# Causal attention: values 256 columns wide, in pieces behind the four long steps, and one turned buffer per query tile

## The reference, cut to what matters

```python
qkv = einsum('bnd,ed->bne', xn, w_qkv)          # xn: layernorm of x; 16 heads of 64
q, k, v = split(qkv, 3)                          # q is scaled by 64 ** -0.5
sim = einsum('bhid,bhjd->bhij', q, k)            # 1024 queries by 1024 keys
sim = where(j > i, -big, sim)                    # causal
attn = softmax(sim)
out = einsum('bhij,bhjd->bhid', attn, v)
x = x + einsum('bne,de->bnd', out, w_out) + b_out
```

## Time and profile before

| | |
|---|---|
| median of 3 executions | 3728.84 us (3725.52 to 3732.86) |
| profiled execution, its own time | 3723.46 us |
| span of the profile, first to last instruction | 3721.7 us |
| mean granted TensorE clock | 0.966 of full speed |
| busy over the span: PE, PEld, DVE, ACT, POOL | 3207.6, 2018.8, 2102.9, 2087.8, 1727.1 us |
| line 1528 (values), PE MATMUL | 4608 instructions, 307.8 us busy, 278 ns each |
| the stretch of `causal_attention`'s units | about 1608 to 2875 us of the span |

### The profile page before, as it was taken

How to read it: one execution, slowest core, us unless ns; L and a number is a source line. 1 busy time by engine, 2 the same in 40 slices (tenths; PEclk the granted TensorE clock), 3 DMA queues, 4 the chain that set the end, 5 groups by cost and what they waited for, 6 DMA issues and landing times. The chain is left out here.

```text
span 3721.7 us, 77077 instructions
## 1 busy us (share of the span) xinstructions
PE 3207.6 (86%) x28486; PEld 2018.8 (54%) x28612; DVE 2102.9 (57%) x4204; ACT 2087.8 (56%) x3388; POOL 1727.1 (46%) x1348
## 2 busy tenths in 40 slices
PE   6599999858889888579999999999998588899885
PEld 4222222635566666346666666666665355666663
DVE  4200000468887777455555555555556688777773
ACT  2499999335555555345555555555554355555552
POOL 1100000168888888223333333333332688888882
PEclk9799999979999999889999999999999799999998
DMA  1122221021111111000000000000000211111111
GB/s 34 22 37 39 36 38 25 7 83 38 34 35 35 35 34 30 14 9 10 6 6 8 6 6 8 6 8 6 6 8 2 85 35 34 35 35 35 34 31 32
DMA packets 124408, 95.75 MB, mean 26 GB/s; under 512 B 80448, under 2 KB 100544, under 8 KB 123968
## 3 DMA queue, kind: packets, MB, share of 16 engines
q1 hardware_dynamic: 122784, 89.41, 11.0%
q10 hardware_dynamic: 1440, 3.80, 0.3%
HBM read 22.90 MB, written 2.10 MB: 7 GB/s over the span
## 5 line engine op out<-in xcount | busy, mean ns | idle before, releaser
L1703 POOL TENSOR_SCALAR e<-e,inv 128x768 f32<-128x768 f32 (+7 forms) x512 | 375.0, 745 | 845.2 <-DVE inv L1599 845.2
L1668 ACT ACTIVATE e<-e,nmax 128x768 f32<-128x768 f32 (+7 forms) x512 | 396.0, 774 | 434.4 <-DVE e L1594 431.2
L530 ACT ACTIVATE e<-slot 128x1024 f32<-128x1024 f32 x512 | 472.6, 1091 | 38.5 <-PE slot L466 38.5
L1594 DVE TENSOR_SCALAR_CACHE_REDUCE e<-slot 128x768 f32<-128x768 f32 (+7 forms) x512 | 375.7, 753 | 161.4 <-PE slot L1504 161.4
L1515 PE MATMUL slot<-ident,e 128*128 128x128 f32 x2304 | 354.7, 281 | 32.5 <-DVE eT L1587 28.2
L880 POOL TENSOR_TENSOR inv_norm<-floored,minus_half 128x16 f32<-128x16 f32 x128 | 374.1, 2923 | 10.7
L1498 PE MATMUL slot<-key,q 64*128 64x512 f32 (+3 forms) x1536 | 317.2, 517 | 38.2 <-DVE e L1594 37.0
L1117 ACT ACTIVATE probT<-slot 128x1024 f32<-128x1024 f32 x128 | 131.0, 1023 | 372.1 <-PE slot L973 372.1
L852 POOL TENSOR_TENSOR prob<-prob,inv_total 128x1024 f32<-128x1024 f32 x128 | 242.7, 1896 | 200.8 <-DVE inv_total L1209 200.8
L873 POOL TENSOR_TENSOR rot<-cosine,sine 128x1024 f32<-128x1024 f32 x128 | 302.0, 2360 | 53.0 <-DVE sine L1191 52.8
L1587 DVE COPY eT<-slot 128x512 f32<-128x512 f32 (+3 forms) x384 | 237.8, 619 | 149.7 <-PE slot L1515 149.7
(11 more groups left out here) (156 smaller groups left out, 6322.1 us busy)
## 6 DMA issues: line engine op xcount, KB each, us to landing
v_mix<-v SPq DMA_DIRECT2D x256, 128.0 KB, 2.3
w_qkv<-in_causal_w_dram SPq DMA_DIRECT2D x32, 192.0 KB
query<-q_hi SPq DMA_DIRECT2D x128, 32.0 KB
keys<-q_hi SPq DMA_DIRECT2D x128, 32.0 KB
query<-q_lo SPq DMA_DIRECT2D x128, 32.0 KB
keys<-q_lo SPq DMA_DIRECT2D x128, 32.0 KB
hs<-H SPq DMA_DIRECT2D x32, 128.0 KB
h1s<-H SPq DMA_DIRECT2D x32, 128.0 KB
```

The lines of the kernel that those rows point to most:

```text
L530: act.activation(e[n % E_RING][:], c.slots[n % RING][:].rearrange(flat), ACT.Exp, scale=2 * SCALE).then_inc(e_ready, 1)
L1594: dve.tensor_scalar(e[n % RING][h][:, 0:cols], c.slots[h][:].rearrange(flat)[:, 0:cols], -1.0, None, ALU.mult, ALU.min, accum_out=nmax[:, ...
L1668: act.activation(part, part, ACT.Exp, bias=nmax[:, n, h:h + 1], scale=-1.0, accum_out=total[:, n, h:h + 1]).then_inc(e_ready, 1)
L1703: pool.tensor_scalar(part, part, inv[:, n, h:h + 1], 1.0, ALU.mult, ALU.mult).then_inc(scaled, 1)
```

## The change

A buffer `eT` is no longer shared by every fourth step. There is one for each pair of steps (0, 2), (1, 3), (4, 6), (5, 7) and head, with room for both query tiles side by side: `[P, 2, tiles, P]`. The values of a pair are then taken together: for the key tiles that both have, one product moves 256 columns (two runs of 128), and one product of 128 columns is left for the last key tile of the longer one (64 instructions of 256 columns and 16 of 128 columns for each unit). The place of the query tiles in the PSUM tile `o` changes with it (even steps in bank 1, odd steps in bank 0).

The values no longer stand behind the second turn of every step. They stand behind that of steps 0, 2, 4 and 6 only (`behind`): in step 0 key tiles 4 and up of pair 0 and all of pair 1 of the unit before (12 instructions of 256 columns and 4 of 128, then 4 and 4); in step 2 pair 2 (20 and 4); in step 4 pair 3 (12 and 4) and then `output` half 0; in step 6 `output` half 1 and then the first four key tiles of pair 0 of the unit itself (16 of 256). The steps 1, 3, 5 and 7 have no values and no output. VectorE's `gather` and `add` move behind `copy_out(n, 1)` of steps 3, 5 and 7. After the last unit the remaining values and outputs follow as before.

```diff
+    PAIR_STEPS = ((0, 2), (1, 3), (4, 6), (5, 7))
-    T_LAG, V_LAG = 2, 3
+    T_LAG = 2
+    def place(n):
+        return 4 * (1 - n % 2) + n // 2
+    def turned_tile(n, h):
+        return eT[n // 4 * 2 + n % 2][h][:, n // 2 % 2]
...
-        eT = [[sb(f"eT{r}{h}", [P, S]) for h in range(2)] for r in range(RING)]
+        eT = [[sb(f"eT{pair}{h}", [P, 2, max(TILES[m] for m in PAIR_STEPS[pair]) + 1, P]) for h in range(2)] for pair in range(4)]
...
+                def values(u, k, pair, part=(0, TPB), first=False):
+                    one, two = PAIR_STEPS[pair]
+                    shared = min(tile_of(one), tile_of(two)) + 1
+                    if pair < 2 and part[0] == 0 and not first:
+                        pe.wait_ge(x_ready, 2 * u - 1 + pair)
+                    if part[0] == 0:
+                        for bank in range(2):
+                            pe.wait_ge(eT_out[bank], chunks(u, two, 1 if wide(two) else bank, bank) + 1)
+                    for t in range(part[0], min(part[1], shared)):
                         for h in range(2):
+                            m = pe.matmul(o[64 * h:64 * h + 64, place(one) // 4, place(one) % 4 * P:(place(one) % 4 + 2) * P],
+                                          v[k][:, t, 64 * h:64 * h + 64], eT[pair][h][:, :, t, :],
+                                          start=(t == 0), stop=False, skip_group_check=True)
+                    if part[1] == TPB:
+                        longer = max(one, two, key=tile_of)
+                        for h in range(2):
+                            m = pe.matmul(o[64 * h:64 * h + 64, place(longer) // 4, place(longer) % 4 * P:(place(longer) % 4 + 1) * P],
+                                          v[k][:, shared, 64 * h:64 * h + 64], turned_tile(longer, h)[:, shared, :],
+                                          start=False, stop=True, skip_group_check=True)
+                    if pair >= 2:
                         m.then_inc(o_ready, 1)
...
+                def behind(u, k, n, first):
+                    if n == 6:
+                        if not first:
+                            output(u - 1, 1 - k, 1)
+                        values(u, k, 0, (0, 4), first)
+                    if first:
+                        return
+                    if n == 0:
+                        values(u - 1, 1 - k, 0, (4, TPB))
+                        values(u - 1, 1 - k, 1, first=(isinstance(u, int) and u == 1))
+                    if n == 2:
+                        values(u - 1, 1 - k, 2)
+                    if n == 4:
+                        values(u - 1, 1 - k, 3)
+                        output(u - 1, 1 - k, 0)
...
-                        trailing(u, k, n, first)
+                        behind(u, k, n, first)
...
-                        if n == 3 and not first:
-                            add(u - 1, 0)
-                        if n in (2, 3) and not first:
-                            gather(u - 1, n - 2)
-                        if n == 4 and not first:
-                            add(u - 1, 1)
...
+                        if n == 3 and not first:
+                            gather(u - 1, 0)
+                        if n == 5 and not first:
+                            gather(u - 1, 1)
+                            add(u - 1, 0)
+                        if n == 7 and not first:
+                            add(u - 1, 1)
```

More of the change, by code:

```diff
@@ L1517, in transpose @@
                         m.then_inc(turned[bank], 1)
[L1519 to L1526, removed]
-                        for h in range(2):
[L1528 to L1531, removed]
+                def values(u, k, pair, part=(0, TPB), first=False):
[7 more added lines that the diff above has]
+                    for t in range(part[0], min(part[1], shared)):
+                        for h in range(2):
+                            m = pe.matmul(o[64 * h:64 * h + 64, place(one) // 4, place(one) % 4 * P:(place(one) % 4 + 2) * P],
[8 more added lines that the diff above has]
+                    if pair >= 2:
                         m.then_inc(o_ready, 1)
@@ L1539, in output @@
                     for t in range(4):
-                        m = pe.matmul(o[:, bank, t * P:(t + 1) * P], oT[:, (4 * bank + t) * P:(4 * bank + t + 1) * P],
+                        at = (7 - t if bank else t) * P
+                        m = pe.matmul(o[:, bank, t * P:(t + 1) * P], oT[:, at:at + P],
                                       wo[k][:], start=True, stop=True)
                     m.then_inc(y_ready, 1)
[L1544 to L1552, removed]
+                def behind(u, k, n, first):
[13 more added lines that the diff above has]
+                        output(u - 1, 1 - k, 0)
                 def unit(u, k, first=False, last=False):
@@ L1572, in _ @@
                 u, k = UNITS - 1, (UNITS - 1) % 2
[L1573 to L1577, removed]
+                for h in range(2):
+                    transpose(u, 6, h, False)
+                values(u, k, 0, (4, TPB))
+                values(u, k, 1)
+                for h in range(2):
+                    transpose(u, 7, h, False)
+                values(u, k, 2)
+                values(u, k, 3)
                 output(u, k, 0)
@@ L1586, in evacuate @@
                             dve.wait_ge(turned[0], chunks(u, n, h, 0) + 1)
-                            dve.tensor_copy(eT[n % RING][h][:, at * P:(at + tiles) * P], turn[:, 0, 0:tiles * P])\
+                            dve.tensor_copy(turned_tile(n, h)[:, at:at + tiles, :].rearrange("p t q -> p (t q)"), turn[:, 0, 0:tiles * P])\
                                .then_inc(eT_out[0], 1)
@@ L1661, in evacuate @@
                             act.wait_ge(turned[1], chunks(u, n, h, 1) + 1)
-                            act.activation(eT[n % RING][h][:, at * P:(at + tiles) * P], turn[:, 1, 0:tiles * P],
+                            act.activation(turned_tile(n, h)[:, at:at + tiles, :].rearrange("p t q -> p (t q)"), turn[:, 1, 0:tiles * P],
                                            ACT.Copy).then_inc(eT_out[1], 1)
```

## The result

The changed kernel takes 3734.6 us, median of 20 executions (3728.06 to 3738.95), against 3727.82 for the kernel before (20 executions). The medians lie 6.8 us apart. The ratio over all executions is 1.0015, which is 5.6 us, with a 95% interval of 1.0008 to 1.0022: a small loss that the interval sets apart from no change, and within the 0.2% that the prediction took as the least that can be told. 3734.6 us lies inside the range of 3704 to 3752 and 5.6 us above the forecast of 3729.

What follows compares the result with a forecast made beforehand. TensorE was taken to bound the stage; stretches of +4.24 and -4.24 us left a unit at 39.3 us, edges added 1, so the profiled 3723.46 us became 3724, and medians 5 higher gave 3729 us, range 3704 to 3752.

Steps and rivals of the forecast that it cites:

- What bounds, and where TensorE waited: TensorE bounds the stage; its 1.9 us a unit of waits, between long steps and the short steps behind them, go.
- The price of values: Value groups of steps 0, 2, 4, 6 take 2.32, 2.53, 1.67, 1.88 us; 0.7 us a unit saved with four groups.
- The filled stretches: Behind long steps 0, 2, 4, 6, now with values: +0.48, +0.57, +1.36, +1.83 us, together +4.24 a unit.
- The empty stretches: Behind short steps 1, 3, 5, 7, now without values and timed by ScalarE: -0.65, -2.35, -0.87, -0.37 us, together -4.24.
- the 0.05 us for the wait to be seen: Estimated delay from the end of ScalarE's work, such as `project_out`, until TensorE starts: about 0.05 us.
- The sum: Over a unit's eight stretches +4.24 and -4.24 us leave nothing; a unit stays at 39.3 us.
- The edges: Unit 0 loses work, the tail behind the last unit gets 2.2 us of values; +1 us for both.
- The new waits are hidden: Rival, 12%: second projections are out in time, scores follow their turn at once; 1.63 us less a unit, 3679 us.
- Values get cheaper: Rival, 10%: group cost and excess over the columns go with the weight loads; 22 us less, 3707 us.
- ScalarE comes late: Rival, 18%: delays of ScalarE in the four empty stretches count in full; 0.22 us in each gives 3756 us.
- The moving operand costs: Rival, 6%: two runs of the moving operand cost extra in 32 pairs a unit; 8 us to 150 us (3880).
- A wait behind a long step stays: Rival, 4%: `copy_out` comes later than 2.91 us behind the values of step 0; 0.5 us a unit, 3744 us.

Runs made afterwards that it cites:

- narrow form: Changed kernel with the shared key tiles taken in two products of 128 columns in place of one of 256: 3735.26 us, 1.0021.
- spare copy: Changed kernel and kernel before, ScalarE copying the slot of every second projection once more before bringing it out: 3778.7 us (1.0144) and 3729.41 us (1.0008).
- other order: Changed kernel and kernel before, ScalarE's second projection directly behind the first, bank 1 before exponential 0 in step 7: 3673.21 us (0.9858) and 3726.25 us (0.9998).
- better order: Changed kernel; ScalarE takes bank 1, second projection, then exponential 1 in steps 1, 3, 5, and bank 1 first in step 7: 3663.74 us, 0.9823.
- projections taken together: Changed kernel; in steps 1, 3 and 5 ScalarE brings out the second projection directly behind the first: 3703.23 us, 0.993.

## Why the prediction was right

**What bounds, and where TensorE waited.** Right: with values behind every long step the waits for VectorE vanished from the listed waits of PE. The new waits are 2.63 us a unit (in the unit shown, six of 0.15 to 0.72 us), not four of some 3 us together, and TensorE is 0.52 us less busy in a unit, not about 1.

**The price of values.** Right to a hundredth: 2.32, 2.52, 1.66 (2424.93 to 2426.59) and 1.88 (2435.84 to 2437.72) against 2.32, 2.53, 1.67 and 1.88. The narrow form in the same places showed 0.08 us a unit for the width, where 0.13 follows from my numbers. What is saved is mostly the groups.

**The filled stretches.** Step 0 took 2.90 (2405.04 to 2407.94) for 2.91; step 2 took 2.52 for 2.53. The others agree within 0.07.

**The empty stretches.** This was the heart of it, and the runs bear it out: the two copies of ScalarE are on the path after the change and not before it (spare copy: 1.0144 and 1.0008; other order: 0.9858 and 0.9998). Each empty stretch was mis-sized a little. The scores of step 2 came 1.70 behind the turn (2410.83 to 2412.53) for 1.62, those of step 4 came 1.48 (2420.93 to 2422.41) for 1.40, those of step 6 came 1.70 (2431.05 to 2432.75) for 1.62. The term that was off is the 0.05 us for the wait to be seen: from the end of `project_out` at 2412.40 to the scores it is 0.13. That is 0.08 in three stretches. In step 7 to 0 it was 2.55 (from the corner at 2399.77 to 2402.32) for 2.48. There the tile that waited went 0.05 behind the end of ScalarE's copy, as taken, and the scores 0.26 behind that tile (2402.06 to 2402.32), not 0.20.

**The sum.** 39.3 us a unit forecast, 39.38 measured over 30 units (1181.28 / 30), against 39.26 (1177.79 / 30, from 1653.65 to 2831.44). That is 3.5 us. In the unit shown the empty stretches came out 0.31 us longer than forecast and the filled ones 0.11 shorter. The stretches said to keep their length gave 0.08, nearly all of it in step 6, where the turn of six tiles ahead of the output took 0.71 (2434.15 to 2434.86) for 0.80. So part of the closeness is luck: misses with opposite signs. The edges: I took +1. The head, from the first scores of unit 0 to those of unit 1, came out 1.7 us shorter (34.40 against 36.13), as the slots of the short steps emptied; the last unit and the tail came out 5.7 us longer (0.73 to the last corner, 4.98 from there to the outputs), of which 1.3 to 1.5 is the clock. So +4, not +1: the mis-sized term of the sum is the tail. I counted the values moved there and not the waits of 0.80 and 1.25 us between the last turns, where the kernel before has one of 0.95, nor the clock. Between the two profiles this makes 7.5 us in the stage; the other 3.6 of the 11.1 between the spans lie in code that the change does not touch (2.2 before the first scores). The ratio over all executions says 5.6 in all, the medians 6.8; and the forecast started from 3728.84, the median of three, where twenty give 3727.82.

**The rivals.** "The new waits are hidden" fell. Its 3679 was passed only when ScalarE's order was changed too (3673.21 and 3663.74), so it is the order, and no slack, that hides them. "Values get cheaper" fell with the narrow form. "ScalarE comes late" did not come about in its form: ScalarE was idle 0.70, 0.37 and 0.41 us before it emptied bank 1 in steps 1, 3 and 5, waiting for TensorE. Its price, though, was the right order of magnitude: half a microsecond more in three steps is 44 us. "The moving operand costs" fell. "A wait behind a long step stays" fell: none is in the waits from 1700 to 2800 us.

## What to carry to other kernels

When work is moved on the bound engine from a place without waits to a place with waits, the emptied place is the thing to cost: take the chain of the other engine from the bound engine's last instruction there to its next, and read every link from rows. What was cover in the old order may be all that hid the order of another engine's queue. So move the queue of that engine with it: first what the bound engine needs next. Here the new placement with its wide products gave +0.15%, an order on ScalarE alone 0, and both together -1.4%. A better order gave -1.8% with the new placement; it was not tried in the kernel before.

## What the runs showed of the hardware

Behind the last unit TensorE's clock fell although it never stood still for long. The waits there, and the windows view of the changed kernel at this place (the last columns are the granted clock, the DMA share and GB/s):

```profile
2869.90 0.33 PE L1524 MATMUL slot<-ident,e 128*128 128x128 f32 x1 [0.80 <-ACT eT L1691]
2871.48 0.83 PE L1524 MATMUL slot<-ident,e 128*128 128x128 f32 x5 [1.25 <-DVE eT L1615]
2872.24 2.83 PE L1539 MATMUL slot<-eT,v 128*64 128x256 f32 x12
2874.85 0.64 PE L1545 MATMUL slot<-eT,v 128*64 128x128 f32 x4
```

```profile
2869.00:2871.00 2.00, 0.43 (x2) 0.14 (x1) 1.25 (x5) 1.71 (x6) 0.22 (x2) 1.00 0.00 0
...
2872.00:2873.00 1.00, 1.00 (x6) 0.53 (x6) 0.69 (x1) 0.28 (x1) 0.30 (x1) 0.50 0.00 0
2873.00:2874.00 1.00, 1.00 (x7) 0.47 (x4) 0.00 (x0) 0.00 (x0) 0.00 (x0) 0.50 0.00 0
```

TensorE was busy 0.43 of 2 us, with single pauses of 0.80 and 1.25, and from 2872 on had the lower level, 1.2 GHz (0.50), for some three microseconds of dense products: the twelve wide instructions took 2.61 us instead of 1.35. The Trainium skill, page "TensorE: Matmul & The Clock Gate", section "Why this matters for your kernels", advises against pauses of more than about 3 us between bursts. No pause here was as long as that. The narrow form, the projections taken together and the spare copy in the changed kernel have the same two pauses at this place, and in each profile the clock fell behind them: four of four, with the one above. With the values ahead of the turns (two pauses of 0.77 us) it stayed full in both profiles. Where bank 1 is emptied first in step 7 there is one pause of 1.95 or 1.96 us. Behind it the clock stayed at 1.00 in two profiles (bank 1 first in step 7, and both orders together) and fell to 0.50 in the third, with the better order, though the work at this place is the same. The twelve wide instructions behind the pause, first with both orders together, then with the better order:

```profile
2812.86 1.52 PE L1539 MATMUL slot<-eT,v 128*64 128x256 f32 x12
```

```profile
2804.38 2.79 PE L1539 MATMUL slot<-eT,v 128*64 128x256 f32 x12
```

So the pauses just ahead do not settle by themselves whether the clock falls, and what does stays open.
